# A feed-forward block's hidden activations: from TensorE transposes to DMA transposes of int16

## The chip, the cores and the metric

The kernel runs on one core of a Trainium2 chip. The metric is the device time of one execution in microseconds (us). Five engines work side by side, each on its own list of instructions: TensorE (PE in the profile, with its weight loads as PEld), VectorE (DVE), ScalarE (ACT), GpSimd (POOL) and SyncE (SP), which only waits and issues DMAs. They are tied together by semaphores that the kernel's author wrote by hand.

## What is computed

The input x has 16 images of 512 channels and 24 x 8 = 192 positions. An attention part comes first, then a feed-forward part over tokens, one token per position:

```
x = x + attention(layernorm_over_channels(x))      # channel gate (fc1, fc2), then a 7x7 gate over positions
t = tokens(x)                                      # 16*192 tokens of 512
t = t + ffn(layernorm(t))
ffn:  h   = bitlinear(x, w1)                       # 512 -> 2048
      h   = gelu(h)
      out = bitlinear(h, w2)                       # 2048 -> 512
bitlinear(x, w): weights rounded to -1, 0, 1 times a scale;
      scale   = 127 / max(|x|) of the token
      x_quant = clip(round(x * scale), -128, 127) / scale
```

So between the two matmuls each token's 2048 Gelu outputs are scaled by 127 / max, rounded to whole numbers from -127 to 127, and multiplied with w2. A matmul contracts over the partitions, so the rounded activations, which lie with a token per partition, must be turned first: 128 tokens by 2048 become 16 blocks of 128 hidden units by 128 tokens.

## The kernel before

Two images make a *pair* of 384 tokens, and a pair makes three *tiles* of 128 tokens (NT = 3). There are 8 pairs (NP). Every engine first runs a start that is written out, then `body(pair, attend, normalise)` once per pair. Body c does four things for four different pairs at once: it finishes the feed-forward part of pair c, starts that of pair c+1 (`nxt`), does the attention of pair c+2 (`att`), and takes in pair c+3 (`fresh`): transposes of x, layernorm statistics. `normalise` is off in body 7 and `attend` in bodies 6 and 7. `attend` also switches `fresh`, so body 5 takes in a ninth pair that nobody uses; SyncE loads pair 6 once more for it (`load_x(Pair(8), source=NP - 2)`).

The way of one tile T through the feed-forward part, with its semaphores:

- VectorE `add_attention` writes t, `centre` writes cen and its scale q1; GpSimd `round_x` (L443) rounds; TensorE `turn_xq` (L1089) transposes; ScalarE copies to xq as f16.
- TensorE `ffn_in` (L1102) makes four blocks of 512 hidden units in PSUM, four matmuls each. The banks are `h_loop`: ps_h0, ps_h1, ps_t1, ps_h0 again.
- ScalarE `gelu` writes g (f32, a tile of `w1_room`, so the profile calls it w_room). VectorE `hidden_max` (L809) takes the maximum of each half, `hidden_scale` (L815 to L822) makes q2.
- GpSimd `round_g` (L448) computes g * q2 + MAGIC in place, 128x2048 f32. The constant leaves the whole number in the low 16 bits of each word.
- TensorE `turn_hq` (L1115) transposes those low halves, 16 blocks, into the PSUM banks ps_t0 and ps_t1. ScalarE `copy_hq` moves them in four copies to hq (f16), subtracting a constant. Behind the second copy it moves a finished output tile (`copy_out`).
- TensorE `ffn_out` (L1125) does 16 matmuls in four quarters into ps_o. VectorE `add_ffn` (L832) adds t and writes res; `turn_res` (L1134) turns it; ScalarE `copy_out` and SyncE `store_out` bring it out.

On TensorE the tiles are staggered: ffn_in of tile T+1, then turn_hq of T, then turn_res of T-1, then ffn_out of T. On ScalarE: gelu of T+1, then copy_hq of T. On VectorE, in the middle of a body: hidden_scale of tile 2, add_ffn of tile 1, attention and centring of the next pair's tile 1, hidden_max of the next pair's tile 0, `hidden` (L731, the fc1 result), hidden_scale, add_ffn of tile 2. Each engine's list is fixed, and a wait holds up all that stands behind it. TensorE's fc1 for the channel gate (L1047) stands inside ffn_out of tile 2, behind its third quarter.

SyncE loads x (`load_x`) and stores outputs (`store_out`); it waits nearly all the time for the next finished output tile.

Of the kernel before, what the change touches and what calls it, by code (L numbers as in the profile page):

```python
# [5 lines left out]
def metaformer_kernel(nc, x, fc1_w, fc2_w, sa_w, w1, w2, out):  # L6
# [38 lines left out]
    with ctx:  # L45
# [107 lines left out]
        h_loop = [ps_h[0][:, :], ps_h[1][:, :], ps_t[1][:, :].bitcast(f32), ps_h[0][:, :]]  # L153
# [77 lines left out]
        h_turned = sem("h_turned")  # L231
# [129 lines left out]
        def _(pool):  # L361
# [104 lines left out]
            def body(pair, attend, normalise):  # L466
                for s in range(NT):
# [3 lines left out]
                    if attend and s == NT - 1:  # L471
# [3 lines left out]
                if attend:  # L475
# [865 lines left out]
```

## Time and profile before

| | |
|---|---|
| median of 3 runs | 332.18 us (331.90 to 332.73) |
| the profiled execution | 332.48 us |
| its span, first to last instruction | 330.7 us |
| TensorE busy | 294.7 us, 2230 matmuls |
| VectorE busy | 278.5 us |
| ScalarE busy | 222.2 us |
| GpSimd busy | 142.5 us |
| 16 transposes of hidden activations per tile | 384, 25.4 us busy |

The profile is one execution. Busy time is the union of an engine's instructions. A matmul's row shows its whole way through the array, and rows overlap, so what a group costs in the stream is read from the start of one row to the start of the next. Body 4, which is used as the example, begins on VectorE and TensorE at about 218 us, body 5 at 252, body 6 at 286, body 7 at 312.

### The profile page before, as it was taken

Reading aid. Unit: us, or ns where it says so; the run is one execution under the profiler, and the core shown is the slowest. Engines: PE = TensorE matmul, PEld = TensorE weight load, DVE = VectorE, ACT = ScalarE, POOL = GpSimd, SP = SyncE. Lnnn points to the kernel's source line nnn. Section 1 sums busy time; section 2 is a strip of 40 time slices with the busy share of each in tenths; the row PEclk is TensorE's granted clock in tenths of the full one; section 3 lists DMA queues with packets and bytes.
Section 4 is the critical chain, followed back from the end, with each engine's and each line's share of the span. In section 5 each row is a group of like instructions: output and inputs, shape, how many; then the busy total and the mean of one; then the engine's idle time right before and its main releaser. Section 6 shows DMA issues by size and latency. Waiting matters only on the chain. (4 is left out here: it accounts for less than half of the span.)

```text
span 330.7 us, 6659 instructions
## 1 busy us (share of the span) xinstructions
PE 294.7 (89%) x2230; PEld 176.0 (53%) x2230; DVE 278.5 (84%) x667; ACT 222.2 (67%) x493; POOL 142.5 (43%) x193
## 2 busy tenths in 40 slices
PE   2458666699999999999999999999999999999994
PEld 2345534646555565646564646464746565555551
DVE  0757989789899989998999899998899899989840
ACT  2286397477775877587658666866686668666662
POOL 7405347223733374337342834184327433653330
PEclk9755679659999999999999999999999999999999
DMA  4999600000001220113010401040104010101103
GB/s 127 318 389 414 182 1 2 0 0 2 4 0 50 61 85 1 50 41 103 2 50 17 128 0 51 0 146 0 50 1 146 2 49 1 50 2 48 48 3 95
DMA packets 21449, 22.44 MB, mean 68 GB/s; under 512 B 1384, under 2 KB 18792, under 8 KB 20904
## 3 DMA queue, kind: packets, MB, share of 16 engines
q1 hardware_dynamic: 19752, 20.98, 19.1%
q10 hardware_dynamic: 1664, 1.05, 1.1%
q8 instruction: 18, 0.29, 0.4%
q14 instruction: 15, 0.12, 0.1%
HBM read 15.73 MB, written 6.29 MB: 67 GB/s over the span
## 5 line engine op out<-in xcount | busy, mean ns | idle before, releaser
L1125 PE MATMUL ps_o<-w2T,hq 128*128 128x512 f16 x384 | 92.6, 380 | 0.0
L1102 PE MATMUL ps_h<-w1T,xq 128*128 128x512 f16 x296 | 74.6, 389 | 0.8 <-ACT xq L491 0.8
L448 POOL TENSOR_SCALAR w_room<-w_room,q 128x2048 f32<-128x2048 f32 x24 | 47.4, 1974 | 62.7 <-DVE q L822 62.7
L491 ACT ACTIVATE w_room<-ps_h,s 128x512 f32<-128x512 f32 x74 | 50.2, 688 | 15.8 <-PE ps_h L1102 13.5
L809 DVE TENSOR_REDUCE amax<-w_room 128x1 f32<-128x1024 f32 x48 | 57.1, 1207 | 1.4 <-ACT w_room L491 1.4
L1125 PEld LDWEIGHTS ps_o<-w2T,hq 128*128 128x128 f16 x384 | 35.0, 98 | 36.9 <-ACT hq L491 3.5
L491 ACT ACTIVATE hq<-ps_t 128x512 f16<-128x512 f16 x96 | 51.4, 608 | 2.4 <-PE ps_t L1115 2.4
L1102 PEld LDWEIGHTS ps_h<-w1T,xq 128*128 128x128 f16 x296 | 27.3, 99 | 32.4 <-issue 2.6
L491 ACT ACTIVATE junk_m<-front 128x192 bf16<-128x192 f32 x64 | 20.5, 327 | 25.2 <-DVE pooled L724 25.0
L782 DVE SCALAR_TENSOR_TENSOR t<-pv,sg,xt 128x512 f32<-128x512 f32 x24 | 31.9, 1328 | 2.7 <-DVE res L832 0.5
L443 POOL TENSOR_SCALAR cen<-cen,q 128x512 f32<-128x512 f32 x24 | 16.6, 691 | 35.9 <-DVE q L804 35.9
L1115 PEld LDWEIGHTS ps_t<-id,w_room 128*128 128x128 f16 x384 | 23.4, 98 | 5.9 <-POOL w_room L448 0.5
L1115 PE MATMUL ps_t<-id,w_room 128*128 128x128 f16 x384 | 25.4, 219 | 0.0
L1027 PE MATMUL front<-id,x_in 128*128 128x128 f32 x108 | 18.9, 310 | 6.5 <-DMA x_in<-in_x 6.0
L711 DVE BATCH_NORM_STATS2 st<-xt 128x6 f32<-128x512 f32 x27 | 17.7, 681 | 7.4 <-ACT xt L491 7.4
L1037 PE MATMUL front<-id,v 128*128 128x128 f32 x96 | 17.7, 305 | 6.3 <-ACT junk_m L491 3.2
L832 DVE SCALAR_TENSOR_TENSOR res<-ps_o,s,t 128x512 f32<-128x512 f32 x24 | 17.8, 740 | 6.4 <-PE ps_o L1125 6.4
L431 POOL TENSOR_SCALAR v<-xt,minus_mean,rs 128x512 f32<-128x512 f32 x27 | 22.1, 823 | 1.6
L1102 PE MATMUL ps_t<-w1T,xq 128*128 128x512 f16 x88 | 22.6, 379 | 0.0
L491 ACT ACTIVATE xt<-front 128x512 f32<-128x512 f32 x27 | 15.6, 597 | 9.9 <-PE front L1027 9.8
L491 ACT ACTIVATE xq<-front 128x512 f16<-128x512 f16 x24 | 14.3, 597 | 9.5 <-PE front L1089 9.5
L1027 PEld LDWEIGHTS front<-id,x_in 128*128 128x128 f32 x108 | 14.4, 159 | 10.3 <-issue 7.6
(126 smaller groups left out, 491.6 us busy)
## 6 DMA issues: line engine op xcount, KB each, us to landing
x_in<-in_x SPq DMA_DIRECT2D x16, 384.0 KB, 5.2
out<-w_room SPq DMA_DIRECT2D x16, 384.0 KB, 2.6
w_room<-in_L_ffn_w SPq DMA_DIRECT2D x4, 1024.0 KB, 9.3
w_raw<-in_L_ffn_w SPq DMA_DIRECT2D x4, 1024.0 KB, 12.3
x_in<-in_x ACTq DMA_DIRECT2D x2, 384.0 KB, 3.9
fc_raw<-in_L_conv_fc_w ACTq DMA_DIRECT2D x2, 128.0 KB, 4.2
taps_rev<-in_L_conv_sa_w SPq DMA_DIRECT2D x2, 0.2 KB
taps_rev<-in_L_conv_sa_w SPq DMA_DIRECT2D x2, 0.3 KB
```

The costliest lines, as they stand in the source:

```text
L431: pool.tensor_scalar(v1[:, s, :], xt[pair.par][:, s, :], minus_mean[:, s:s + 1], rs1[:, s:s + 1], ALU.add, ALU.mult).then_inc(normed, 1)
L448: pool.tensor_scalar(c[:, :], c[:, :], q2[tile.par][:, 0:1], MAGIC, ALU.mult, ALU.add).then_inc(g_rounded, 1)
L491: act.activation(out_ap, in_ap, func, **more).then_inc(signal, 1)
L711: chain.mark(dve.bn_stats(st1[:, s, :], xt[pair.par][:, s, :]))
L782: link(dve.scalar_tensor_tensor(t_tile, pv[par][:, s, :], sg[par][:, s:s + 1], xt[par][:, s, :], ALU.mult, ALU.add))
L809: chain.mark(dve.tensor_reduce(amax2[:, i:i + 1], g[tile.par][:, i * F // 2:(i + 1) * F // 2], AX.X, ALU.max, apply_absolute_value=True))
L832: dve.scalar_tensor_tensor(res[tile.par][:, :], ps_o[:, :], s2[tile.par][:, 0:1], t[tile.pair.par][:, tile.s, :], ALU.mult, ALU.add).then_ ...
L1027: last = pe.transpose(front[bank][:, tile_cols(k)], x_in[tile.pair.par][:, k, tile_cols(tile.s)], id32[:, :])
L1037: last = pe.transpose(front[bank][:, tile_cols(s)], v1[:, s, tile_cols(k)], id32[:, :])
L1102: last = pe.matmul(banks[b], xq[tile.pair.par][:, tile.s, k, :], w1T[:, k, b * 512:(b + 1) * 512], start=(k == 0), stop=(k == NC - 1))
L1115: last = pe.transpose(ps_t[i][:, tile_cols(k)], q[:, tile_cols(i * NF // 2 + k)], id16[:, :])
L1125: last = pe.matmul(ps_o[:, :], hq[tile.par][:, k, :], w2T[:, k, :], start=(k == 0), stop=(k == NF - 1))
```

## The change

Four edits:

1. `round_g` writes g * q2 as int16 into another buffer, g_int, without the constant; the conversion does the rounding. g_int and the turned hq_int are in the room of the raw w2 weights (`w2_raw`, w_raw in the profile), which is free once those are transposed.
2. `turn_hq` and its 16 transposes per tile go. SyncE gets `turn_h`: it waits for the round (and for the casts of the tile two before) and issues two DMA transposes, each 128 tokens by 1024 hidden units into 8 blocks of 128x128, with a semaphore of its own for each half and buffer. `copy_hq` is now two casts of 128x1024 from int16 to f16, one for each half, with `copy_out` between them.
3. `ps_t` no longer holds transposes in the loop, so `h_loop` has four different banks, and block b of ffn_in waits for the Gelu of block b of the tile before.
4. A fourth argument `turn` of `body` switches the part on `fresh`. It is off from body 5 on, and the load of the ninth pair goes.

```diff
+        g_int = [w2_raw[:, 0, i * F // 2:(i + 1) * F // 2].bitcast(i16) for i in range(2)]
+        hq_int = [w2_raw[:, 1, i * F // 2:(i + 1) * F // 2].bitcast(i16).rearrange("p (k q) -> p k q", q=P)
+                  for i in range(2)]
...
-        h_loop = [ps_h[0][:, :], ps_h[1][:, :], ps_t[1][:, :].bitcast(f32), ps_h[0][:, :]]
+        h_loop = [ps_h[0][:, :], ps_h[1][:, :], ps_t[0][:, :].bitcast(f32), ps_t[1][:, :].bitcast(f32)]
...
+            def turn_h(tile):
+
+                wait(sp, w_turned, 12)
+                wait(sp, g_rounded, tile.at(1, 1))
+                wait(sp, hq_ready, tile.at(2, -2))
+                for half in range(2):
+                    cols = slice(half * NF // 2, (half + 1) * NF // 2)
+                    sp.dma_start_transpose(hq_int[tile.par][:, cols, :],
+                                           g_int[tile.par][:, half * F // 2:(half + 1) * F // 2]
+                                           ).then_inc(h_turned[tile.par][half], 16)
+
+            turn_h(Tile(Pair(0), 0))
+            turn_h(Tile(Pair(0), 1))
+            for c in range(NP):
+                turn_h(Tile(Pair(c), 2))
+                if c < NP - 3:
+                    load_x(Pair(c + 3))
+                if c < NP - 1:
+                    turn_h(Tile(Pair(c + 1), 0))
                 store_out(Pair(c))
-            load_x(Pair(7))
-            store_out(Pair(4))
-
-            load_x(Pair(8), source=NP - 2)
...
+                if c < NP - 1:
+                    turn_h(Tile(Pair(c + 1), 1))
...
             def round_g(tile):
+                wait(pool, w_turned, 10)
                 wait(pool, q2_ready, tile.at(1, 1))
-                c = g[tile.par]
-                pool.tensor_scalar(c[:, :], c[:, :], q2[tile.par][:, 0:1], MAGIC, ALU.mult, ALU.add).then_inc(g_rounded, 1)
+                for half in range(2):
+                    wait(pool, h_turned[tile.par][half], tile.turns(-1))
+                pool.tensor_scalar(g_int[tile.par], g[tile.par][:, :], q2[tile.par][:, 0:1], None,
+                                   ALU.mult).then_inc(g_rounded, 1)
...
-                wait(act, h_turned, tile.at(2, -2))
+                wait(act, g_rounded, tile.at(1, -1))
...
-                for i in range(4):
-                    wait(act, h_turned, tile.at(2, i // 2 + 1))
-                    copy(hq[tile.par][:, i * NF // 4:(i + 1) * NF // 4, :],
-                         ps_t[i // 2][:, i % 2 * 512:(i % 2 + 1) * 512].rearrange("p (k q) -> p k q", q=P),
-                         hq_ready, bias=-F16_ZERO)
-                    if i == 1 and out_tile:
+                wait(act, o_done, tile.at(1, -1))
+                for half in range(2):
+                    wait(act, h_turned[tile.par][half], tile.turns())
+                    cols = slice(half * NF // 2, (half + 1) * NF // 2)
+                    copy(hq[tile.par][:, cols, :], hq_int[tile.par][:, cols, :], hq_ready)
+                    if half == 0 and out_tile:
                         copy_out(out_tile, out_bank)
...
-                free = {0: 0, 3: 1} if banks is h_loop else {b: b - 1 for b in range(FB)}
+                if banks is h_start:
+                    before = [-1, 0, 1, 2]
+                else:
+                    before = [-1, 0, 0, 0] if tile.at() == 2 else [-3, -2, -1, 0]
                 for b in blocks:
-                    if b in free:
-                        wait(pe, g_ready, tile.at(FB, free[b]))
+                    wait(pe, g_ready, tile.at(FB, before[b]))
...
-                turn_hq(Tile(pair, 1), Tile(pair, 2))
                 a = turn_res(Tile(pair, 0), OUT_BANK[0], a)
...
-            for c in range(6):
-                body(Pair(c), True, True)
-            body(Pair(6), False, True)
-            body(Pair(7), False, False)
+            for c in range(NP):
+                body(Pair(c), c < NP - 2, c < NP - 1, c < NP - 3)
```

TensorE, middle of body 0, from the last blocks of ffn_in of the next pair's tile 0 to ffn_out of tile 2. front<-id,res are the res transposes, front<-id,v those of the attention's v1. Before:

```order
L1102 MATMUL ps_h<-w1T,xq 128x512 [waits g_ready]
L1102 MATMUL ps_h<-w1T,xq 128x512 x3
L1115 MATMUL ps_t<-id,w_room 128x128 [waits hq_ready,g_rounded]
L1115 MATMUL ps_t<-id,w_room 128x128 x7
L1115 MATMUL ps_t<-id,w_room 128x128 [waits g_ready,hq_ready]
L1115 MATMUL ps_t<-id,w_room 128x128 x7
L1134 MATMUL front<-id,res 128x128 [waits xq_ready,res_ready]
L1134 MATMUL front<-id,res 128x128 x3
```

The same place after:

```order
L1126 MATMUL ps_t<-w1T,xq 128x512 [waits g_ready]
L1126 MATMUL ps_t<-w1T,xq 128x512 x3
L1146 MATMUL front<-id,res 128x128 [waits xq_ready,res_ready]
L1146 MATMUL front<-id,res 128x128 x3
L1059 MATMUL front<-id,v 128x128 [waits mean_ready,normed]
L1059 MATMUL front<-id,v 128x128 x2
L1137 MATMUL ps_o<-w2T,hq 128x512 [waits res_ready,hq_ready]
```

The sixteen transposes and their wait on g_rounded are gone from TensorE; only ffn_out still waits for the activations, through hq_ready.

ScalarE, the same place: the Gelu blocks of the next pair's tile 0 (w_room<-ps), then what brings tile 2 to hq. Before:

```order
L491 ACTIVATE w_room<-ps_t,s_0 128x512 [waits h_done]
L491 ACTIVATE w_room<-ps_h,s_0 128x512 [waits h_done]
L491 ACTIVATE hq<-ps_t 128x512 [waits h_turned] x2
L491 ACTIVATE w_room<-front 128x4x128 [waits out_stored1,res_turned]
L491 ACTIVATE hq<-ps_t 128x512 [waits h_turned] x2
L491 ACTIVATE junk_m,pooled<-front 128x192 [waits mean_ready,max_ready]
```

After:

```order
L511 ACTIVATE w_room<-ps_t,s_0 128x512 [waits h_done] x2
L511 ACTIVATE hq<-w_raw 128x1024 [waits h_turned1_0,o_done]
L511 ACTIVATE w_room<-front 128x4x128 [waits out_stored1,res_turned]
L511 ACTIVATE hq<-w_raw 128x1024 [waits h_turned1_1]
L511 ACTIVATE junk_m,pooled<-front 128x192 [waits mean_ready,max_ready]
```

Two casts stand where four copies stood, each behind its half's DMA; the output copy is still between them.

SyncE, after the start: loads and stores before, with what stands there now behind it.

```order
L320 DMA x_in<-in_x 128x4x192 [waits x_turned]
L320 DMA x_in<-in_x 128x4x192
L325 DMA out<-w_room 128x4x192 [waits out_ready] x2
L320 DMA x_in<-in_x 128x4x192 [waits x_turned]
L320 DMA x_in<-in_x 128x4x192
```

```order
L360 DMA_TRANSPOSE w_raw<-w_raw 128x8x128 [waits hq_ready,g_rounded,w_turned]
L360 DMA_TRANSPOSE w_raw<-w_raw 128x8x128
L327 DMA x_in<-in_x 128x4x192 [waits x_turned]
L327 DMA x_in<-in_x 128x4x192
L360 DMA_TRANSPOSE w_raw<-w_raw 128x8x128 [waits hq_ready,g_rounded,w_turned]
L360 DMA_TRANSPOSE w_raw<-w_raw 128x8x128
L332 DMA out<-w_room 128x4x192 [waits out_ready] x2
L360 DMA_TRANSPOSE w_raw<-w_raw 128x8x128 [waits hq_ready,g_rounded,w_turned]
L360 DMA_TRANSPOSE w_raw<-w_raw 128x8x128
```

Three pairs of transposing DMAs per body have come between the loads and stores, on the same queue.

## Rows read from the trace of the kernel before

**Rows 1.** The page: busy by engine; one group (busy us, mean ns, idle before).

```profile
PE 294.7 (89%) x2230; PEld 176.0 (53%) x2230; DVE 278.5 (84%) x667; ACT 222.2 (67%) x493; POOL 142.5 (43%) x193
...
L711 DVE BATCH_NORM_STATS2 st<-xt 128x6 f32<-128x512 f32 x27 | 17.7, 681 | 7.4 <-ACT xt L491 7.4
```

**Rows 2.** Stretches: busy of PE, PEld, DVE, ACT, POOL; granted clock; DMA share.

```profile
214.80:248.60 33.80, 33.13 (x259) 19.40 (x258) 30.90 (x78) 24.34 (x59) 15.34 (x22) 1.00 0.16 48
...
282.00:330.70 48.70, 44.08 (x320) 23.54 (x318) 33.74 (x75) 28.21 (x52) 19.56 (x23) 0.99 0.13 41
```

**Rows 3.** Waits of VectorE, 114.7 to 282 us: total, times, longest.

```profile
DVE lim L798 <- POOL rs L419: 4.6, 5, 0.9
DVE t L782 <- DVE res L832: 0.5, 1, 0.5
```

**Rows 4.** Waits of TensorE's matmuls, 114.7 to 282 us.

```profile
PE front L1037 <- ACT junk_m L491: 1.4, 5, 0.3
PE small L1059 <- DVE ca_split L742: 1.2, 5, 0.3
```

**Rows 5.** Timeline of TensorE in body 4: start, length, instruction, count.

```profile
231.80 1.06 PE L1115 MATMUL ps_t<-id,w_room 128*128 128x128 f16 x16
232.69 0.61 PE L1134 MATMUL front<-id,res 128*128 128x128 f32 x4
...
233.47 2.75 PE L1125 MATMUL ps_o<-w2T,hq 128*128 128x512 f16 x12
...
236.37 0.63 PE L1047 MATMUL small<-pooled,fc1T 128*64 128x4 f32 x8
```

**Rows 6.** Timeline of VectorE in body 4.

```profile
219.78 0.75 DVE L782 SCALAR_TENSOR_TENSOR t<-pv,sg,xt 128x512 f32<-128x512 f32 x1
...
230.16 1.37 DVE L782 SCALAR_TENSOR_TENSOR t<-pv,sg,xt 128x512 f32<-128x512 f32 x1
...
237.32 0.14 DVE L731 TENSOR_SCALAR hid_r<-small 64x4 f32<-64x4 f32 x1
...
238.20 0.75 DVE L832 SCALAR_TENSOR_TENSOR res<-ps_o,s,t 128x512 f32<-128x512 f32 x1
```

**Rows 7.** Timeline of GpSimd in body 4: the round of tile 2.

```profile
229.01 1.98 POOL L448 TENSOR_SCALAR w_room<-w_room,q 128x2048 f32<-128x2048 f32 x1 [3.24 <-DVE q L822]
```

**Rows 8.** Timeline of ScalarE: body 4, and a weight copy in the start.

```profile
232.00 0.69 ACT L491 ACTIVATE w_room<-ps_h,s 128x512 f32<-128x512 f32 x1
...
233.54 0.61 ACT L491 ACTIVATE w_room<-front 128x512 f32<-128x512 f32 x1
...
70.35 1.11 ACT L491 ACTIVATE w2T<-ps_t,sharp_bias 128x1024 f16<-128x1024 f16 x1 [0.81 <-PE ps_t L1156]
```

**Rows 9.** DMA: landing (us); packets, MB, engines' share, 95:110, then 0:8 us.

```profile
x_in<-in_x SPq DMA_DIRECT2D x16, 384.0 KB, 5.2
out<-w_room SPq DMA_DIRECT2D x16, 384.0 KB, 2.6
...
q1 hardware_dynamic: 528, 0.39, 7.8%
...
q1 hardware_dynamic: 147, 0.00, 1.2%
```

**Rows 10.** Timeline of GpSimd and TensorE: start, then bodies 6 and 7.

```profile
72.12 1.98 POOL L448 TENSOR_SCALAR w_room<-w_room,q 128x2048 f32<-128x2048 f32 x1 [6.99 <-DVE q L822]
...
77.34 1.90 PE L1125 MATMUL ps_o<-w2T,hq 128*128 128x512 f16 x8
...
308.19 2.76 PE L1125 MATMUL ps_o<-w2T,hq 128*128 128x512 f16 x12
...
316.89 3.63 PE L1125 MATMUL ps_o<-w2T,hq 128*128 128x512 f16 x16
...
318.45 1.97 POOL L448 TENSOR_SCALAR w_room<-w_room,q 128x2048 f32<-128x2048 f32 x1 [3.31 <-DVE q L822]
...
321.85 3.62 PE L1125 MATMUL ps_o<-w2T,hq 128*128 128x512 f16 x16
```

More of the change, by code:

```diff
@@ L230, in metaformer_kernel @@
         g_rounded = sem("g_rounded")
-        h_turned = sem("h_turned")
+        h_turned = [[sem(f"h_turned{i}_{half}") for half in range(2)] for i in range(2)]
         hq_ready = sem("hq_ready")
@@ L265, in at, with turns @@
                 return self.pair.at(NT * k, self.s * k + more)
+            def turns(self, more=0):
+                return 16 * (self.at() // 2 + 1 + more)
         SQUARES_BY_VECTOR = [(2,), (2, 3)]
@@ L464, in _, with body @@
             normalise1(Pair(2), 0, 1, 2)
-            def body(pair, attend, normalise):
+            def body(pair, attend, normalise, turn):
                 for s in range(NT):
@@ L470, in body @@
                         round_x(Tile(pair.plus(1), s))
-                    if attend and s == NT - 1:
+                    if turn and s == NT - 1:
                         normalise1(pair.plus(3), 0)
@@ L630, in _, with body @@
             copy_x(Tile(pair2, 2), 0)
-            def body(pair, attend, normalise):
+            def body(pair, attend, normalise, turn):
                 nxt, att, fresh = pair.plus(1), pair.plus(2), pair.plus(3)
@@ L671, in body @@
                     copy_xq(Tile(nxt, 2), XQ_BANK[2])
-                if attend:
+                if turn:
                     copy_x(Tile(fresh, 2), X_BANK[2])
-            for c in range(6):
-                body(Pair(c), True, True)
-            body(Pair(6), False, True)
-            body(Pair(7), False, False)
+            for c in range(NP):
+                body(Pair(c), c < NP - 2, c < NP - 1, c < NP - 3)
         @block.vector
@@ L955, in _, with body @@
             aggregate(pair2, 0, 1, 2)
-            def body(pair, attend, normalise):
+            def body(pair, attend, normalise, turn):
                 nxt, att, fresh = pair.plus(1), pair.plus(2), pair.plus(3)
@@ L1008, in body @@
                     hidden_scale(Tile(nxt, 1))
+                if turn:
+                    channel_stats(fresh, 1, 2)
                 if attend:
-                    channel_stats(fresh, 1, 2)
                     sum_conv(att)
+                if turn:
                     aggregate(fresh, 1, 2)
-            for c in range(6):
-                body(Pair(c), True, True)
-            body(Pair(6), False, True)
-            body(Pair(7), False, False)
+            for c in range(NP):
+                body(Pair(c), c < NP - 2, c < NP - 1, c < NP - 3)
         @block.tensor
@@ L1104, in ffn_in @@
                     last.then_inc(h_done, 1)
-            def turn_hq(tile, last_in=None):
-                wait(pe, g_rounded, tile.at(1, 1))
-                q = low_halves(g[tile.par][:, :])
-                for i in range(2):
-                    wait(pe, hq_ready, tile.at(4, 2 * i - 2))
-                    if i == 1 and last_in:
-                        wait(pe, g_ready, last_in.at(FB, 3))
-                    for k in range(NF // 2):
-                        last = pe.transpose(ps_t[i][:, tile_cols(k)], q[:, tile_cols(i * NF // 2 + k)], id16[:, :])
-                    last.then_inc(h_turned, 1)
             def ffn_out(tile, quarters):
                 for i in quarters:
-                    wait(pe, hq_ready, tile.at(4, i + 1))
+                    wait(pe, hq_ready, tile.at(2, i // 2 + 1))
                     if i == 0:
@@ L1247, in _, with body @@
             conv(pair1)
[L1249 removed]
+            def body(pair, attend, normalise, turn):
                 nxt, att, fresh = pair.plus(1), pair.plus(2), pair.plus(3)
                 a = [(xq_ready, pair.at(NT, NT))]
[L1255 removed]
+                b = [(xt_ready, att.at(NT, NT))] if attend else [(scaled, NP * NT), (out_ready, pair.at(NT))]
                 if attend:
@@ L1310, in body @@
                     ffn_out(Tile(nxt, 0), (3,))
+                if turn:
+                    b = turn_x(Tile(fresh, 2), X_BANK[2], b)
                 if attend:
-                    b = turn_x(Tile(fresh, 2), X_BANK[2], b)
                     conv(att)
-            for c in range(6):
-                body(Pair(c), True, True)
-            body(Pair(6), False, True)
-            body(Pair(7), False, False)
+            for c in range(NP):
+                body(Pair(c), c < NP - 2, c < NP - 1, c < NP - 3)
 _INS = ["x", "L0_conv_fc1_w", "L0_conv_fc2_w", "L0_conv_sa_w", "L0_ffn_w1", "L0_ffn_w2"]
```

24 lines of the change are left out of this document (10 added, 14 removed).

## The prediction

> **What bounds the kernel now.** I read the busy shares first [rows 1], then busy time by stage [rows 2], then who waits in the steady loop [rows 3, 4], then the timeline of one pair [rows 5 to 8]. The whole-span shares mislead: TensorE has 89%, VectorE 84%. By stage it looks different. In the period of pair 4 (33.8 us) VectorE is busy 30.9 us and TensorE 33.1; in the last 48.7 us VectorE is down to 33.7 and TensorE has 44.1 [rows 2]. In 167 us of the loop VectorE waits only 5.1 us, 4.6 of it for GpSimd's small power and 0.5 behind its own res write; it waits for TensorE nowhere [rows 3]. TensorE's matmuls wait 2.6 us, behind ScalarE's junk_m and VectorE's ca_split, never behind a Gelu that frees a bank, nor behind a rounded g [rows 4]. So in bodies 0 to 5 two engines run nearly without gaps, and VectorE's list is the one that cannot shrink: taking work off TensorE alone moves nothing there. After the attention part ends (from about 277 us) TensorE sets the pace: a tile takes 316.89 - 308.19 = 8.70 us [rows 10].
>
> **The change, part by part.**
>
> *The transposes go.* 16 per tile stand between the first matmul and the next res transposes. They begin at 231.80 and the res transposes behind them at 232.69, so they hold the stream for 0.89 us; the second matmul begins at 233.47 [rows 5]. 24 x 0.89 = 21.4 us of TensorE, but in bodies 0 to 5 that is no gain (above), and in the tail it is weighed below.
>
> *What takes their place is latency.* The new path of a tile is: round on GpSimd, SyncE's wait and issue, transposing DMA (two halves of 128x1024, 256 KB), a ScalarE cast of 128x1024, second matmul. I call a the time from the end of the round until the first half has landed, b the same for the second half.
> - Cast: ScalarE's 128x1024 f16 row took 1.11 us [rows 8]; two are 2.2, where four copies were there before. ScalarE has room (24.3 of 33.8 us busy [rows 2]).
> - Round: 1.98 us [rows 7]. No row writes 16 bits from GpSimd; I keep 1.98. Bounds: half of it if only bytes written counted, and half as much again if the conversion costs.
> - a from below: a store of 384 KB lands in 2.6 us [rows 9]. Its 512 packets (768 B) take 0.078 x 15 us x 16 / 528 = 35 ns each, so 512/16 x 35 ns = 1.1 us is movement and 1.5 us is fixed. 256 KB at that rate: 1.5 + 0.75 = 2.2 us.
> - a from above: 128 partitions times 8 blocks make 1,024 pieces of 256 B. At 35 ns each: 64 x 35 ns = 2.2, a = 3.8 us. With the smallest packets of the trace (about 20 B, 0.012 x 8 us x 16 / 147 = 10 ns) as the other support, 256 B would take 18 ns, a = 2.7. The pair of x loads, 5.2 us, is the farthest row that I let count [rows 9]. I take a = 3.3, the middle of 2.7 and 3.8, because the number of pieces and not the bytes differs from the store. b = a + 1.7, one more half's movement (1.2 to 2.3).
>
> The Trainium skill (Advanced Engine Details and Errata, X-Bar Transpose) says that transposing DMAs run as fast as ordinary ones; by it a is at my lower end and the time near 338. The Trainium skill (VectorE: DVE Perf Modes, The three transpose paths) gives the crossbar 1309 ns for one 128x128 block against 390 ns for TensorE, which speaks against the swap: added up over eight blocks it would be 10 us for a half and the third rival below. No row here shows a transposing DMA.
>
> *Steady loop, tile 2 of a pair* (pair 4, the tightest place). The round ends at 229.01 + 1.98 = 230.99 [rows 7]. First half lands 234.3; ScalarE's last Gelu block is done at 232.7 [rows 8], so the cast runs 234.3 to 235.4. TensorE is free for the second matmul at 233.47 - 0.89 = 232.6 and waits until then. Two quarters of 0.86 us (a quarter of sixteen matmuls, whose row is 3.63 us with the last one's drain [rows 10]) end at 237.2. The second cast comes behind the output copy (0.6 [rows 8]) and b = 5.0: 236.0 to 237.1; the third quarter is done at 238.05. Then the transposes of xq (0.3) and fc1 (0.55 [rows 5]): 238.85. VectorE's hid_r stood at 237.32 [rows 6] and nothing it does next can be done first: it now waits until 238.9, **1.6 us a pair**. The last quarter ends at 239.7, its res at 238.20 + 1.6 = 239.8 needs no further wait. The other two tiles have over a microsecond more between their round and their second matmul; I count 0.1 for both. Six bodies: 6 x 1.7 = **+10.2**.
>
> *Start.* The first round ends at 72.12 + 1.98 = 74.1; + 3.3 + 1.1 gives a second matmul at 78.55 instead of 77.34 [rows 10], and VectorE's first add hangs on it: **+1.2**.
>
> *Tail.* ScalarE casts tile T behind the Gelu of tile T+1. From the end of ffn_in to the second matmul it was 0.89 of transposes and 0.44 of res; it is now 0.1 + 0.69 of Gelu [rows 8] + 1.1 + 0.1 of cast = 2.0, with res inside it. So a tile takes 8.70 - 1.33 + 2.0 = 9.37 us even if the transposing costs nothing. Two such tiles put the last round 1.3 late: 318.45 + 1.3 + 1.97 = 321.7, + 3.3 + 1.15 = 326.2 against 321.85 [rows 10]: **+4.3**.
>
> *The banks* of ffn_in: no wait on a Gelu stands in rows 4, so 0. *The ninth pair*: three bn_stats at 0.68 [rows 1] and their small companions leave VectorE in body 5, with 3 x 4 transposes of TensorE; about half lies ahead of the first add of body 6 and the rest under TensorE's chain: **-0.8**.
>
> *Sum:* 1.2 + 10.2 + 4.3 - 0.8 = 14.9. The profiled execution took 332.48 us (span 330.7, 1.8 around it), 0.3 above the median: 332.48 + 14.9 = 347.4, as a median **347 us**.
> Ends: a = 2.2, b = 3.4: 0.5 + 6 x 0.5 + 3.2 - 0.8 = 5.9, **338**. a = 3.8, b = 6.1: 1.7 + 6 x 2.7 + 4.8 - 0.8 = 21.9, **354**. a = 5.2, b = 7.5: hid_r is 4.0 late, and tile 1 loses its cover too (a token maximum waits 1.5 more): 3.1 + 33 + 6.2 - 0.8 = 41, **373**.
>
> **Rivals.**
> 1. *The transpose is as quick as a plain move* (a up to 2.6): 338, 336 to 342. For it: the data never leave SBUF. Against: twice the pieces of the store.
> 2. *Faster.* VectorE's t reads two SBUF operands and takes 0.75 us when GpSimd does something small, 1.37 us when the round is under way: it ends 0.5 us behind the round's end [rows 6, 7]. The Trainium skill (SBUF — State Buffer, SBUF: two separate sides) calls this an exclusive lock for the whole instruction; the trace agrees. If the round with its 16-bit output takes 1.0 us instead of 1.98, two t's a pair give back 0.6 to 0.7 each on the engine that bounds, 1.3 x 6 = 7.8, and every landing comes 1 us sooner: with a at 2.2 the loop's stall is gone, the tail keeps 3.2 - 1, and 332.2 + 2.2 - 7.8 - 0.8 = 326. It decides from a round below some 1.4 us together with a below 2.5; one alone gives no gain. No row shows a shorter round.
> 3. *The transposes queue.* Six halves must pass in each period. If a half holds the queue for more than 33.8 / 6 = 5.6 us, the DMA queue is the bound. Were the 1,024 pieces served one after another through one crossbar at 10 ns, a half would take 10 us and the kernel 74 + 48 x 10.2 + 8 = 572. Against: other DMAs spread over 16 engines. Everything slow goes here, 362 upwards.
> 4. *No difference*: with a below 1.5 the loop's stall is gone and the tail's +1.3 and the ninth pair's -0.8 nearly cancel. 333.
>
> **Chances.** Forecast (343 to 361) 0.58; rival 1 0.18; rival 3 0.14; rival 2 0.06; rival 4 0.04. The likeliest gives 347. The range 336 to 370 leaves out 0.10 below and some 0.10 above. A measurement of this kernel tells 0.3% from no change: faster 0.06, same 0.04, slower 0.58 + 0.18 + 0.14 = 0.90.
>
> **What would show each step.** The landing time of the transposes (a, b). VectorE's waits in the loop: new ones on fc1 ahead of hid_r of 1 to 2 us per pair; if none, the 10.2 falls. TensorE's idle time ahead of the second matmul, released by ScalarE's cast; none on Gelu in ffn_in. Tail tiles 9.4 us apart. The cast at 1.1 and the round at 1.98; t no shorter than before. TensorE's granted clock is 1.00 in the loop and 0.99 in the tail [rows 2]; new waits might let it fall, which I count at nothing. The prediction is wrong if a is under 2 us and the round gets shorter, or if a half takes over 5 us.

## The result, and the profile after

The changed kernel takes **456.97 us** (median of 4, 456.57 to 458.78), the kernel before it 332.46 on the same chip: a ratio of 1.376, 95% interval 1.372 to 1.380. The prediction said 347 us, 336 to 370, with 0.90 for slower. The direction was right and the size was not: 124.5 us more instead of 15. Single executions that took over 1.5% longer than the fastest of the same kernel are left out of the medians below: three of e_f16_round, two of e_banks, one of e_warm.

The page of the kernel after: span, busy time of each engine, the granted clock in 40 slices, four of the costliest groups, and the median landing of the new DMA. The round is now L469, ffn_out L1137, the cast L511, VectorE's t L801.

```profile
span 454.6 us, 5884 instructions
PE 318.8 (70%) x1834; PEld 167.5 (37%) x1834; DVE 318.8 (70%) x661; ACT 223.4 (49%) x442; POOL 219.7 (48%) x184
PEclk9656579798868976976976976976976976979898
L469 POOL TENSOR_SCALAR w_raw<-w_room,q 128x2048 int16<-128x2048 f32 x24 | 130.7, 5445 | 117.4 <-DVE q L841 83.1
L1137 PE MATMUL ps_o<-w2T,hq 128*128 128x512 f16 x384 | 131.2, 498 | 72.4 <-ACT hq L511 72.3
L511 ACT ACTIVATE hq<-w_raw 128x1024 f16<-128x1024 int16 x48 | 50.5, 1054 | 73.4 <-DMA w_raw<-w_raw 72.8
L801 DVE SCALAR_TENSOR_TENSOR t<-pv,sg,xt 128x512 f32<-128x512 f32 x24 | 53.2, 2217 | 2.5 <-DVE res L851 0.5
w_raw<-w_raw SPq DMA_TRANSPOSE x48, 3.2
```

TensorE executes 396 instructions fewer than in [rows 1] and is busy 24 us longer; VectorE has six fewer and is busy 40 us longer. The first group says where to look: GpSimd's round takes 5.445 us, not the 1.98 of [rows 7]. The DMA, which rival 3 put at 10 us a half, lands in 3.2 us.

Tile 2 of pair 4, from the timelines of GpSimd, VectorE, ScalarE, TensorE and again VectorE (start, length, instruction, the idle time before it and who ended it):

```profile
251.68 5.44 POOL L469 TENSOR_SCALAR w_raw<-w_room,q 128x2048 int16<-128x2048 f32 x1 [5.31 <-issue]
252.96 2.97 DVE L801 SCALAR_TENSOR_TENSOR t<-pv,sg,xt 128x512 f32<-128x512 f32 x1
260.52 1.06 ACT L511 ACTIVATE hq<-w_raw 128x1024 f16<-128x1024 int16 x1 [4.76 <-DMA w_raw<-w_raw]
261.63 5.16 PE L1137 MATMUL ps_o<-w2T,hq 128*128 128x512 f16 x12 [5.84 <-ACT hq L511]
267.60 0.15 DVE L750 TENSOR_SCALAR hid_r<-small 64x4 f32<-64x4 f32 x1 [5.78 <-PE small L1069]
```

The stretch of its second matmul, with the columns of [rows 2]; the granted clock is the third figure from the end:

```profile
261.60:266.00 4.40, 4.37 (x11) 1.63 (x12) 0.23 (x1) 2.14 (x6) 0.00 (x0) 0.50 0.64 183
```

The round ends at 257.12, the cast begins 3.40 us later (the a of the prediction, 3.3), the matmul follows, at half clock, and VectorE's hid_r has stood still for 5.8 us, where 1.6 was forecast. The waits between 140 and 400 us (five pairs; total, times, longest) put that wait first on VectorE, and show two that [rows 3] does not have:

```profile
DVE hid_r L750 <- PE small L1069: 27.8, 5, 5.8
...
DVE pv L768 <- PE front L1089: 11.1, 5, 3.3
DVE pooled L743 <- PE front L1059: 8.9, 6, 2.2
```

### The profile page after: what moved, and what is told of

Read it like the earlier page. It is cut to its first block and busy times, and to the rows that moved or that the text cites. A ratio compares the mean times of both kernels' runs of the same rounds, so it can differ in the third digit from the quotient of the medians.

```text
span 454.6 us, 5884 instructions
## 1 busy us (share of the span) xinstructions
PE 318.8 (70%) x1834; PEld 167.5 (37%) x1834; DVE 318.8 (70%) x661; ACT 223.4 (49%) x442; POOL 219.7 (48%) x184
## 2 busy tenths in 40 slices
DMA packets 71078, 34.20 MB, mean 75 GB/s; under 512 B 52040, under 2 KB 68424, under 8 KB 70536
## 3 DMA queue, kind: packets, MB, share of 16 engines
q10 hardware_dynamic: 1664, 1.05, 0.9%
## 5 line engine op out<-in xcount | busy, mean ns | idle before, releaser
L469 POOL TENSOR_SCALAR w_raw<-w_room,q 128x2048 int16<-128x2048 f32 x24 | 130.7, 5445 | 117.4 <-DVE q L841 83.1
L1137 PE MATMUL ps_o<-w2T,hq 128*128 128x512 f16 x384 | 131.2, 498 | 72.4 <-ACT hq L511 72.3
L1137 PEld LDWEIGHTS ps_o<-w2T,hq 128*128 128x128 f16 x384 | 42.6, 120 | 139.9 <-ACT hq L511 81.6
L511 ACT ACTIVATE hq<-w_raw 128x1024 f16<-128x1024 int16 x48 | 50.5, 1054 | 73.4 <-DMA w_raw<-w_raw 72.8
L801 DVE SCALAR_TENSOR_TENSOR t<-pv,sg,xt 128x512 f32<-128x512 f32 x24 | 53.2, 2217 | 2.5 <-DVE res L851 0.5
L1126 PE MATMUL ps_h<-w1T,xq 128*128 128x512 f16 x208 | 52.1, 393 | 1.1 <-ACT xq L511 0.7
L1126 PE MATMUL ps_t<-w1T,xq 128*128 128x512 f16 x176 | 43.0, 382 | 0.0
L511 ACT ACTIVATE w_room<-ps_h,s 128x512 f32<-128x512 f32 x52 | 35.1, 690 | 12.0 <-PE ps_h L1126 11.1
L511 ACT ACTIVATE junk_m<-front 128x192 bf16<-128x192 f32 x64 | 20.4, 326 | 30.2 <-DVE pooled L743 30.2
L511 ACT ACTIVATE w_room<-ps_t,s 128x512 f32<-128x512 f32 x44 | 30.3, 688 | 9.2 <-PE ps_t L1126 8.7
L511 ACT ACTIVATE xq<-front 128x512 f16<-128x512 f16 x24 | 14.3, 597 | 37.5 <-PE front L1111 37.2
L768 DVE CUSTOM_DVE_ANT_0 pv<-v,front 128x512 f32<-128x512 f32 x24 | 15.9, 682 | 14.6 <-PE front L1089 14.6
L743 DVE TENSOR_REDUCE pooled<-front 128x2 f32<-128x384 f32 x32 | 17.6, 550 | 11.3 <-PE front L1059 11.0
L1126 PEld LDWEIGHTS ps_t<-w1T,xq 128*128 128x128 f16 x176 | 16.7, 98 | 20.1
```

The lines of the kernel that those rows point to most:

```text
L469: pool.tensor_scalar(g_int[tile.par], g[tile.par][:, :], q2[tile.par][:, 0:1], None, ALU.mult).then_inc(g_rounded, 1)
L511: act.activation(out_ap, in_ap, func, **more).then_inc(signal, 1)
L743: dve.tensor_reduce(pooled[:, k, 0:2], front[bank][:, 0:TOK].rearrange("p (i t) -> p i t", i=2), AX.X, ALU.max).then_inc(max_ready, 1)
L768: dve.tensor_tensor_reduce(out=pv[tile.pair.par][:, tile.s, :], in0=v1[:, tile.s, :], in1=front[bank][:, :], scale=1.0, scalar=-3.0e38, op ...
L801: link(dve.scalar_tensor_tensor(t_tile, pv[par][:, s, :], sg[par][:, s:s + 1], xt[par][:, s, :], ALU.mult, ALU.add))
L1126: last = pe.matmul(banks[b], xq[tile.pair.par][:, tile.s, k, :], w1T[:, k, b * 512:(b + 1) * 512], start=(k == 0), stop=(k == NC - 1))
```

## The experiments

For all of them I use one ruler: the start of hid_r, once per pair on VectorE. From its third to its eighth occurrence are five periods; what is ahead is the start, what is behind the tail. The last four columns are of the profiled execution alone; that of e_warm_after was its fastest, 441.8 us.

| kernel | median us | to the 3rd hid_r | mean period | behind the 8th | span |
|---|---|---|---|---|---|
| before | 332.5 | 102.25 | 33.77 | 59.6 | 330.7 |
| after | 457.0 | 116.88 | 50.60 | 84.7 | 454.6 |
| e_two_ops | 363.3 | 105.99 | 37.48 | 67.0 | 360.4 |
| e_one_op | 403.1 | 110.86 | 43.23 | 73.6 | 400.6 |
| e_one_op_8 | 449.8 | 117.27 | 49.51 | 83.3 | 448.1 |
| e_warm | 356.7 | 104.88 | 36.24 | 69.7 | 355.8 |
| e_warm_after | 444.5 | 114.70 | 48.47 | 82.8 | 439.8 |

**A short round in the changed kernel.** What does the new path cost if the round stays as it was?

```diff
-                pool.tensor_scalar(g_int[tile.par], g[tile.par][:, :], q2[tile.par][:, 0:1], None,
-                                   ALU.mult).then_inc(g_rounded, 1)
+                c = g[tile.par]
+                pool.tensor_scalar(c[:, :], c[:, :], q2[tile.par][:, 0:1], MAGIC, ALU.mult, ALU.add).then_inc(g_rounded, 1)
```

> The changed kernel, but GpSimd's round writes f32 in place with the constant, as before the change (1.97 us a tile there). The DMAs still turn the 16-bit words of g_int, which nothing writes now: what goes into the second matmul is left out of the computation, its timing stays. Theory A (the 5.45 us of the int16 round carry the loss: they lengthen each tile's path by 3.5 us and hold VectorE's t): 345 to 352, the 347 that was forecast for a round of 1.97 us and a landing of 3.3 us. Rival B (the DMAs' latency and the casts carry it): still above 420. Rival C (TensorE's granted clock, 0.804 over the span against 0.932, carries it and falls with any stall): above 390 with a granted clock under 0.85.

The DMAs here turn words that nothing writes; the right activations are left out.

Measured: 363.84 us, ratio 1.096 (1.092 to 1.100), 12 us above theory A's upper end and far below both rivals. So 93 us of the 125 go with the round, and the rest is still twice the forecast. Its round and its first cast, tile 2 of pair 4 (GpSimd, ScalarE):

```profile
249.41 1.97 POOL L470 TENSOR_SCALAR w_room<-w_room,q 128x2048 f32<-128x2048 f32 x1 [3.54 <-issue]
...
254.77 1.06 ACT L511 ACTIVATE hq<-w_raw 128x1024 f16<-128x1024 int16 x1 [1.54 <-DMA w_raw<-w_raw]
```

a is 254.77 - 251.38 = 3.39 us. The path's price per tile was right; what it does to the loop was not.

**Is it the int16 output?** The kernel before, with an int16 output and two operations; TensorE turns those words (the diff leaves out the buffers and their waits).

```diff
-                c = g[tile.par]
-                pool.tensor_scalar(c[:, :], c[:, :], q2[tile.par][:, 0:1], MAGIC, ALU.mult, ALU.add).then_inc(g_rounded, 1)
+                pool.tensor_scalar(g_int[tile.par], g[tile.par][:, :], q2[tile.par][:, 0:1], 26112.0, ALU.mult, ALU.add).then_inc(g_rounded, 1)
```

> The kernel before, but GpSimd's round writes int16 into a buffer of its own (with 26112 added, so that the 16 bits are those of the f16 number that TensorE turned before); TensorE transposes and ScalarE copies as before, no DMA transposes. Theory A: the round takes 5.4 us here too; per pair VectorE's three t's end 3.4 us later each, so 6 to 7 bodies cost some 10 us and the tail 3.4 us a tile: 405 to 425. Rival B: VectorE and TensorE absorb most of it, below 370.

Measured: 332.99 us, ratio 1.0031 (1.0018 to 1.0044). My first theory fell: its group on the page has int16 out and 1.977 us.

```profile
L451 POOL TENSOR_SCALAR w_raw<-w_room,q 128x2048 int16<-128x2048 f32 x24 | 47.4, 1977 | 63.9 <-issue 51.7 <-DVE q L825 12.1
```

**The changed kernel with a 16-bit float round of two operations.** `ALU.mult, ALU.add` with 1536 into f16; the cast takes the constant off again.

> The changed kernel, but the round writes f16 (times scale, plus 1536, which rounds to a whole number in f16) and ScalarE's cast takes 1536 off. If the conversion to an integer is what GpSimd does slowly, the round takes about 2 us and the kernel 345 to 352; if every 16-bit output is slow, the round stays near 5.4 us and the kernel near 457.

Its four executions took 359.69, 365.97, 368.08 and 368.92 us; the kernel before takes 331.84 on the same chip. The round took 1.978 us, so a 16-bit output is not slow by itself. The path costs some 28 us again by the fastest of the four, above the 345 to 352 that was expected; with this spread I take no finer number from this run.

**Which form is slow?** Eight instructions on GpSimd, one after another, behind the end of the kernel before.

> The kernel before with eight more GpSimd instructions of 128x2048 behind its last round, nothing else beside them on GpSimd: to f32 with multiply and add, to f32 with multiply, to int16 with multiply, to int16 with multiply and add, to f16 with multiply and add, to bf16 with multiply, to int32 with multiply, and a plain copy f32 to int16. Theory A: all integer outputs take 5.4 us, the float ones 2. Rival: all 16-bit outputs take 5.4 us and int32 takes 2. Rival: the instruction with one operation instead of two is the slow one, also to f32. The kernel's own time grows by what they take beyond the end, to 345 to 360.

One execution, 353.89 us. The timeline of GpSimd; in the program's order: f32 with multiply and add, f32 multiply only, int16 multiply only, int16 multiply and add, f16 multiply and add, bf16 multiply only, int32 multiply only, a plain copy to int16.

```profile
321.45 1.98 POOL L488 TENSOR_SCALAR w_raw<-w_room,q 128x2048 f32<-128x2048 f32 x1 [1.29 <-PE ps_t L1129]
323.52 5.45 POOL L489 TENSOR_SCALAR w_raw<-w_room,q 128x2048 f32<-128x2048 f32 x1
329.07 5.44 POOL L490 TENSOR_SCALAR w_raw<-w_room,q 128x2048 int16<-128x2048 f32 x1
334.60 1.98 POOL L491 TENSOR_SCALAR w_raw<-w_room,q 128x2048 int16<-128x2048 f32 x1
336.67 1.98 POOL L492 TENSOR_SCALAR w_raw<-w_room,q 128x2048 f16<-128x2048 f32 x1
338.74 5.44 POOL L493 TENSOR_SCALAR w_raw<-w_room,q 128x2048 bf16<-128x2048 f32 x1
344.27 5.44 POOL L494 TENSOR_SCALAR w_raw<-w_room,q 128x2048 int32<-128x2048 f32 x1
349.78 1.89 POOL L495 CAST w_raw<-w_room 128x2048 int16<-128x2048 f32 x1
```

All with two operations take 1.98 us (f32, int16, f16), all with one 5.44 (f32, int16, bf16, int32). The one operation was each time a multiplication by q2; others were not tried. The change dropped the added constant, and with it the second operation.

**The changed kernel with a second operation that does nothing.**

```diff
-                pool.tensor_scalar(g_int[tile.par], g[tile.par][:, :], q2[tile.par][:, 0:1], None,
-                                   ALU.mult).then_inc(g_rounded, 1)
+                pool.tensor_scalar(g_int[tile.par], g[tile.par][:, :], q2[tile.par][:, 0:1], 0.0,
+                                   ALU.mult, ALU.add).then_inc(g_rounded, 1)
```

> The changed kernel with one constant changed: the round to int16 multiplies by the scale and adds 0.0 instead of only multiplying. Theory A (GpSimd's form with one operation is the slow one, whatever it writes): the round takes 1.98 us and the kernel 360 to 368, as in the run with the f32 round in place. Rival (the output's place or type matters in this kernel): 5.4 us and about 457.

Measured: 363.28 us, ratio 1.096 (1.093 to 1.100). One added zero takes off 93.7 us. The group of the round on its page:

```profile
L469 POOL TENSOR_SCALAR w_raw<-w_room,q 128x2048 int16<-128x2048 f32 x24 | 47.4, 1974 | 92.7 <-DVE q L841 67.5 <-issue 25.2
```

The timeline of TensorE: the second matmul of pair 4's tile 2, and two ffn_out at the end.

```profile
250.84 4.31 PE L1137 MATMUL ps_o<-w2T,hq 128*128 128x512 f16 x12 [2.62 <-ACT hq L511]
...
342.49 3.67 PE L1137 MATMUL ps_o<-w2T,hq 128*128 128x512 f16 x16 [1.29 <-ACT hq L511]
...
350.10 5.04 PE L1137 MATMUL ps_o<-w2T,hq 128*128 128x512 f16 x16 [2.44 <-ACT hq L511]
```

The stretch of the first of these, and the one behind it:

```profile
250.00:254.50 4.50, 3.66 (x10) 1.38 (x11) 2.74 (x4) 2.84 (x7) 0.69 (x1) 0.62 0.64 186
254.70:258.00 3.30, 3.30 (x30) 2.39 (x27) 1.62 (x7) 0.60 (x1) 0.90 (x1) 1.00 0.00 0
```

VectorE's wait from 125 to 300 us:

```profile
DVE hid_r L750 <- PE small L1069: 16.8, 5, 3.8
```

The twelve matmuls took 2.75 us in [rows 5] and 4.31 here. They follow a wait of 2.6 us, and the granted clock of their window is 0.62, a mixture of the chip's 1.2 and 2.4 GHz. So hid_r waits 16.8 / 5 = 3.4 us a pair instead of 1.6; that is nearly all of the 3.7 us by which a period is longer. The last ffn_out, behind a wait of 2.4 us, takes 5.04 where [rows 10] has 3.62; the one behind a wait of 1.3 takes 3.67.

**The slow round alone, on the kernel before.** TensorE still turns (the diff leaves out the buffer, its waits and the constant that ScalarE no longer takes off).

```diff
-                pool.tensor_scalar(c[:, :], c[:, :], q2[tile.par][:, 0:1], MAGIC, ALU.mult, ALU.add).then_inc(g_rounded, 1)
+                pool.tensor_scalar(g_f16[tile.par], g[tile.par][:, :], q2[tile.par][:, 0:1], None, ALU.mult).then_inc(g_rounded, 1)
```

> The kernel before, with GpSimd's round as one multiplication to f16 in a buffer of its own, which TensorE turns and ScalarE copies without the constant; the rounding to whole numbers is left out. So only the slow form is added, with no DMA transpose. Theory A (the round's 3.5 us more lie on the path and hold VectorE's t, which waits for GpSimd's instruction to end): 8 to 11 us a pair in the loop and 3.5 us at the last tile, 400 to 425. Rival (the round is covered and the loss needs the DMA path as well): below 350.

Measured: 403.06 us, ratio 1.213 (1.209 to 1.217), 71.1 us more for 24 x 3.47 = 83.3 us of longer rounds: 0.85 of each added microsecond reaches the end. Its round and VectorE's t beside it:

```profile
241.77 5.45 POOL L450 TENSOR_SCALAR w_raw<-w_room,q 128x2048 f16<-128x2048 f32 x1 [5.32 <-issue]
...
242.50 3.53 DVE L784 SCALAR_TENSOR_TENSOR t<-pv,sg,xt 128x512 f32<-128x512 f32 x1
```

t takes 0.75 us undisturbed [rows 6]. It looks as if that were the whole cost: VectorE is held while GpSimd is at its instruction. The next run says no.

**The slow round in eight pieces.** If the held t were the cost, t could slip in between pieces (the diff leaves out the same parts).

```diff
-                pool.tensor_scalar(g_f16[tile.par], g[tile.par][:, :], q2[tile.par][:, 0:1], None, ALU.mult).then_inc(g_rounded, 1)
+                for part in range(8):
+                    cols = slice(part * F // 8, (part + 1) * F // 8)
+                    last = pool.tensor_scalar(g_f16[tile.par][:, cols], g[tile.par][:, cols], q2[tile.par][:, 0:1], None, ALU.mult)
+                last.then_inc(g_rounded, 1)
```

> The kernel before with the one-operation round (403.1 us when it is one instruction of 5.44 us), now cut into eight instructions of 128x256, 0.7 us each, one signal behind the last; TensorE turns as before. As there, the constant and so the rounding to whole numbers is left out. Theory A (most of the 71 us is VectorE held until the GpSimd instruction under way ends): t can start between two pieces and is back near 1.4 us (3.2 in the uncut form), and what stays is the round's longer way, 5.6 instead of 2.0 us, which a path with 5.6 us more of latency in the int16 version with a short round priced at 31 us in all: 345 to 360 us. Theory B (the cost is the late end of the round for TensorE and ScalarE, not the held VectorE): the round ends no sooner, 395 to 410 us.

Measured: 449.79 us, ratio 1.354 (1.350 to 1.358): 47 us slower than uncut, outside both theories. A piece takes 0.92 us and not 0.68, so a tile's round takes 179.7 / 24 = 7.49 us. Two groups of its page:

```profile
L452 POOL TENSOR_SCALAR w_raw<-w_room,q 128x256 f16<-128x256 f32 x192 | 179.7, 954 | 80.2 <-issue 70.3
L803 DVE TENSOR_SCALAR lim<-amax,rs 128x1 f32<-128x1 f32 x24 | 5.1, 214 | 95.7 <-POOL rs L420 95.7
```

All t of the run (duration ns min/median/max, first and last start), and one line of VectorE's timeline:

```profile
L787 DVE SCALAR_TENSOR_TENSOR t<-pv,sg,xt x24: 750/753/2196, 40.3 to 414.0; 128x512 f32<-128x512 f32 x24
...
245.96 0.21 DVE L803 TENSOR_SCALAR lim<-amax,rs 128x1 f32<-128x1 f32 x1 [5.24 <-POOL rs L420]
```

t is back at 0.75 us: that half of theory A holds. But VectorE now waits 95.7 us in all for rs, GpSimd's small power for the same token's layernorm, which stands behind the round on GpSimd's list. In the kernel before the same wait has 7.4 us over the whole run, 4.6 of them in [rows 3], the largest of VectorE there. So VectorE cannot pass the end of the round in either form: held at t, or stopped one step later at lim. The rounds are 24 x (7.49 - 1.98) = 132 us longer and the kernel 117.7: 0.89 of each microsecond, as without the pieces.

**Is the clock a cause?** Forty transposes of a constant, which nobody reads, fill TensorE's wait ahead of ffn_out of tile 2 in e_two_ops.

```diff
+                if 0 in quarters and tile.s == 2:
+                    for _ in range(40):
+                        pe.transpose(small[:, 64:128].bitcast(f16), id16[:, :], id16[:, :])
                 for i in quarters:
                     wait(pe, hq_ready, tile.at(2, i // 2 + 1))
```

> The changed kernel with the two-operation round and 40 transposes of a constant into an unused corner of PSUM ahead of the second matmul of each pair's tile 2, where TensorE waited 2.6 us for the cast and then ran at a granted clock of 0.59. Theory A' (the second part of the miss is TensorE's clock after the wait): the clock stays at 1.00 there, twelve matmuls take 2.6 us instead of 4.45, VectorE's wait at hid_r falls from 3.4 to 1.6 us, and the kernel takes 8 to 11 us less than without them: 351 to 357. Rival (the clock falls for another reason, or the wait itself is what counts): 362 or more.

Measured: 356.68 us, ratio 1.0746 (1.0715 to 1.0776), 6.6 less than without, where 8 to 11 were expected. TensorE's timeline at the same place:

```profile
243.97 2.40 PE L1134 MATMUL small<-id 128*128 128x128 f16 x40
...
246.75 2.76 PE L1140 MATMUL ps_o<-w2T,hq 128*128 128x512 f16 x12 [0.39 <-ACT hq L511]
```

VectorE's wait from 125 to 300 us:

```profile
DVE hid_r L750 <- PE small L1069: 9.1, 5, 2.4
```

More work on TensorE, and the kernel is faster: the twelve matmuls are back at 2.76 us, the wait at 1.8 us a pair, near the forecast's 1.6. Yes, the clock is a cause. By the ruler the filler shortens start and loop by 7.3 us and lengthens the tail by 2.7: there, at another tile, a burst without a filler now stands behind a wait of 2.55 us and takes 4.45. The length of the wait does not decide alone: a few tiles later twelve matmuls behind a wait of 2.48 us took 2.76, at a granted clock of 1.00.

```profile
308.61 4.45 PE L1140 MATMUL ps_o<-w2T,hq 128*128 128x512 f16 x12 [2.55 <-ACT hq L511]
...
330.31 2.76 PE L1140 MATMUL ps_o<-w2T,hq 128*128 128x512 f16 x12 [2.48 <-ACT hq L511]
```

**The same filler in the changed kernel itself**, 80 there and 50 ahead of the first v1 transposes, where it stood still for 3.7 us.

> The changed kernel, round of 5.44 us included, with idle TensorE time filled by transposes of a constant that nobody reads: 80 in front of the second matmul of a pair's tile 2 (it stood still for 5.8 us there and then ran at a granted clock of 0.50), 50 in front of the first v1 transposes (3.7 us still). Theory A (the clock adds to the stalls): the 12 matmuls behind the first filler take 2.75 us instead of 5.16, the 12 behind the second 2.6 instead of 4.9; where fc1 is late for VectorE that is 2.4 us a pair, and a part of the other: 6 x 2.4 = 14 to 6 x 4.5 = 27 us less, 430 to 443 us. Theory B (the clock is a symptom; VectorE and the round set the end): within 3 us of 457, or above where a filler is in the way.

Measured: 444.5 us (441.8 to 447.76), ratio 1.339 (1.332 to 1.347): 12.5 less than the changed kernel, just outside the 430 to 443 of theory A, far from theory B. TensorE at the two places:

```profile
235.80 2.96 PE L1277 MATMUL small<-id 128*128 128x128 f16 x50
...
248.89 4.63 PE L1134 MATMUL small<-id 128*128 128x128 f16 x80
255.12 2.99 PE L1140 MATMUL ps_o<-w2T,hq 128*128 128x512 f16 x12 [1.61 <-ACT hq L511]
```

Twelve matmuls now take 2.99 us instead of 5.16. The fillers at these two places take back 12.5 us; what the clock costs elsewhere in the changed kernel was not tried.

**The banks.** e_two_ops with the banks and waits of the kernel before (the diff leaves out the waits):

```diff
-        h_loop = [ps_h[0][:, :], ps_h[1][:, :], ps_t[0][:, :].bitcast(f32), ps_t[1][:, :].bitcast(f32)]
+        h_loop = [ps_h[0][:, :], ps_h[1][:, :], ps_t[1][:, :].bitcast(f32), ps_h[0][:, :]]
```

> The changed kernel with the two-operation round and the first matmul's banks and waits as before the change (ps_h0, ps_h1, ps_t1, ps_h0 again). What the prediction said of the banks, 0: within 0.5% of the run with four banks. Rival (four banks let the first matmul run ahead of the Gelus): 2 to 5 us slower.

Measured: 361.9 and 362.0 us, where e_two_ops took 362.4 to 365.4. The four banks give nothing.

**The ninth pair.** The kernel before with only the fourth edit of the change.

> The kernel before without the ninth pair, and nothing else of the change. The prediction gave it -0.8 us: 331.1 to 331.8 beside 332.2 for the kernel before (ratio 0.997 to 0.999). Rival (nothing of it lies on the path): within 0.1 us.

Measured: 331.19 us against 331.95, ratio 0.9972 (0.9962 to 0.9982): 0.8 us less, as forecast.

**A version that beats both.** The kernel before without the ninth pair, and with the round in two halves, each with its own signal, so that TensorE turns the first half earlier (the diff shows GpSimd's part only):

```diff
-                c = g[tile.par]
-                pool.tensor_scalar(c[:, :], c[:, :], q2[tile.par][:, 0:1], MAGIC, ALU.mult, ALU.add).then_inc(g_rounded, 1)
+                for half in range(2):
+                    c = g[tile.par][:, half * F // 2:(half + 1) * F // 2]
+                    pool.tensor_scalar(c, c, q2[tile.par][:, 0:1], MAGIC, ALU.mult, ALU.add).then_inc(g_rounded, 1)
```

> The kernel before without the ninth pair, and with GpSimd's round in two halves of 128x1024, each with its own signal; TensorE's transposes of the first half wait for the first alone. VectorE's t ends 0.5 us behind GpSimd's instruction when the two overlap; with a shorter instruction it can start between the halves. If that holds, t takes 0.8 to 1.1 us instead of 1.4 two times a pair, up to 1 us a pair on the engine that bounds: 325 to 330. Rival (TensorE, busy 33.1 of 33.8 us, takes over as the bound, or the second half holds t just the same): 330 to 333.

Measured: 329.04 us, ratio 0.9909 (0.9890 to 0.9928), 2.2 below the ninth pair's edit alone. Two groups of its page:

```profile
L448 POOL TENSOR_SCALAR w_room<-w_room,q 128x1024 f32<-128x1024 f32 x48 | 56.7, 1195 | 69.3 <-DVE q L819 69.3
...
L779 DVE SCALAR_TENSOR_TENSOR t<-pv,sg,xt 128x512 f32<-128x512 f32 x24 | 26.2, 1091 | 2.5 <-DVE res L829 0.5
```

GpSimd works 9 us more (2.39 us a tile), and the mean t is 0.24 us shorter: 5.7 us off VectorE's list. How the 2.2 us divide between that and the earlier transposes was not tried. By the ruler a period falls only from 33.77 to 33.58 us, though three t's of a pair are 0.7 us shorter together: a shorter list of VectorE does not come out in full in this loop, where TensorE is busy for 33.1 us of a period too [rows 2].

## Why the prediction was right in direction and wrong in size

*What bounds it: right for what is added, and not read to the end.* Waits added to VectorE's list lengthen the loop nearly one for one (3.4 of 3.7 us a pair in e_two_ops). The prediction noted that its largest wait was for GpSimd's small power [rows 3], 4.6 us, and drew nothing from it. It is one wait a pair, at tile 0. VectorE's and GpSimd's timelines of body 4 in the kernel before, at tile 0 and at tile 1:

```profile
224.07 0.21 DVE L798 TENSOR_SCALAR lim<-amax,rs 128x1 f32<-128x1 f32 x1 [0.93 <-POOL rs L419]
...
232.57 0.48 POOL L418 TENSOR_SCALAR ve<-mv 128x1 f32<-128x1 f32 x1 [1.57 <-DVE mv L786]
```

At tile 0 GpSimd works without a pause from a round at 217.65 to this rs at 223.41, so a longer round ahead comes out on VectorE. At tiles 1 and 2 GpSimd still stands idle for 1.57 us between the round and the power. There the row alone would not have told the price: the held t passes the time on (e_one_op), and where t is free (e_one_op_8) 1.57 us is less than the 5.5 us that the round grew. The two runs measured the price for all three tiles: 0.85 and 0.89 of each added microsecond.

*The round: the step that failed.* "I keep 1.98. Bounds: half of it ... and half as much again if the conversion costs." It took 5.44. The row behind the 1.98 is of another form, one with two operations, and the prediction did not ask what dropping the constant makes of it. Its bounds looked at the output type, which turned out to cost nothing. By e_one_op this term alone is 71 us, where the sum had 0. Rival 2 had the right chain, from round to t, but only its good side was priced: a shorter round. The same chain with a round of 3 us would have been a slow rival of some 24 x 1 x 0.85 = 20 us more (an estimate).

*The Trainium skill* (SBUF — State Buffer, SBUF: two separate sides) says that whoever has the shared ports blocks the other for its whole instruction. The traces agree in part. Held t's of 3 to 3.5 us beside a round of 5.44 are there, but t ends at 255.93, 1.2 us ahead of the round's end at 257.12 (at 246.03 against 247.22 in e_one_op); and beside eight pieces that follow each other within 0.1 us it took 0.75 us. The runs do not show why.

*The transposing DMA: right.* a was 3.4 for 3.3, and the second half went without a wait of its own that mattered: in the changed kernel its cast began at 262.42, 5.3 us behind the round's end, for b = 5.0. Rivals 1 and 3 are out. The number of pieces was right too: packets under 512 B rise from 1,384 to 52,040 on the page, some 1,055 for each of the 48 halves, where the prediction had 1,024. *The cast*: 1.05 for 1.11.

*Steady loop: the mechanism right, the term too small.* With the round at 1.98 (e_two_ops) a period is 37.48 - 33.77 = 3.7 us longer, against 1.7. VectorE waits on fc1 ahead of hid_r, exactly as told, but 3.4 us. The missing part is what the last paragraph of the prediction named and "counted at nothing": the clock. A wait of 2.6 us ahead of the second matmul brings twelve matmuls from 2.75 to 4.31 us. With the filler the wait is 1.8 us. What is left of the period, 36.24 against 35.5 forecast, is as large as VectorE's new waits at pv for TensorE's spread, 3.5 us in five pairs. They stand in e_warm, in e_fast_round with 1.4 us, and in e_two_ops not at all; where they come from was not tried.

*Tail:* tiles 324.30 to 333.46 to 342.49, 9.16 and 9.03 us, for 9.37 forecast and 8.70 before. The last one failed by the same clock: 5.04 for 3.62. Tail and ninth pair together were forecast at +3.5 and came to +7.4; the start (with the first of the six bodies) at +2.9 and came to +3.7. These are single profiled executions: that of e_fast_round, 364.67 us, has +8.0 in the start and +4.5 in the tail. *Banks* 0 and *ninth pair* -0.8: right.

*The two misses together.* In spans, the slow round alone costs 69.9 us, the rest of the change with a short round 29.7, sum 99.6; the changed kernel 123.9. The excess of 24.3 lies in the loop for 18.3. There a pair's hid_r waits 27.8 / 5 = 5.6 us, against 3.4 in e_two_ops and 1.5 at pair 4 of e_one_op. My reading is that each cost alone used up slack that the other then did not find, and that longer stalls lower the clock further (0.50). The clock's part has a number: the fillers, at two places a pair, take off 12.5 us here, and the one of e_warm 6.6 there, so about 6 of the 24 us. The rest was not taken apart, and its cause stays open.

*Range:* 336 to 370 held e_two_ops at 363, not the kernel. It missed because one price without a row got bounds of a factor 1.5 where the truth was 2.75.

## What to carry to other kernels

When an edit drops an operand or an operation, treat the instruction as a new one without a price: the nearest row is of another form, and the bounds must be wide, or the old form kept (adding 0.0 was worth 93.7 us here). Look at what stands behind a lengthened instruction on its own engine before blaming what is held beside it, and at the idle time between the two: here it was none at one tile of three and 1.57 us at the others, and 0.85 to 0.89 of the added time came out. And a new wait ahead of a burst of matmuls can be paid twice, once standing still and once in the clock behind it: in e_two_ops waits of 1.3 to 1.9 us ahead of twelve or sixteen matmuls cost nothing more, waits of 2.4 us and up did, and in e_warm one of 2.48 did not.

## What the runs showed of the hardware

- GpSimd's tensor_scalar on 128x2048 f32 takes 1.98 us with two operations (f32, int16 and f16 outputs), 5.44 with one (f32, int16, f16, bf16 and int32 outputs); a plain copy to int16 takes 1.89. At 128x256 the form with one takes 0.92, at 128x1024 the form with two 1.19.
- A transposing DMA of 128x1024 two-byte words within SBUF lands in 3.2 us in the median (3.1 to 4.9), the store of 384 KB in 2.6 [rows 9]; this agrees better with the Trainium skill's sentence that transposing DMAs run as fast as others (Advanced Engine Details and Errata, X-Bar Transpose) than with eight times its 1309 ns for one block (VectorE: DVE Perf Modes, The three transpose paths).
- Behind a wait of 1.3 us sixteen matmuls took 3.67 us, behind 2.4 us 5.04; twelve behind 2.6 us took 4.31 (granted clock 0.62), behind 5.8 us 5.16 (0.50), and 2.76 with the wait of 2.6 filled; behind 1.9 us (e_two_ops) and once behind 2.48 us (e_warm) they took 2.76 without a filler just ahead. Four behind 1.27 us took 1.04 us five times and 1.89 once (e_two_ops).
